# A gated delta-rule decoder layer: the inverse of the triangular blocks up to 16 rows by substitution on GpSimd, with the triangle in two buffers and a new order of steps

## What is computed

```python
def step(S, inp):
    qt, kt, vt, gt, bt = inp
    S = S * jnp.exp(gt)[..., None, None]
    kv = jnp.einsum('bhk,bhkv->bhv', kt, S)
    delta = (vt - kv) * bt[..., None]
    S = S + jnp.einsum('bhk,bhv->bhkv', kt, delta)
    o = jnp.einsum('bhk,bhkv->bhv', qt, S)
    return (S, o)
```

## Time and profile before

| | us |
|---|---|
| three runs: lowest, median, highest | 2253.6, 2258.28, 2272.47 |
| the profiled execution | 2256.81 |
| its span in the trace | 2255.0 |

### The profile page before, as it was taken

The page is one execution under the profiler, slowest core; times in us unless marked ns, Lnnn a source line. Parts: engine busy times, 40 slices in busy tenths (PEclk is TensorE's granted clock), DMA queues, the critical chain, the costliest instruction groups (busy, mean ns, idle before and its releaser), DMA issues.

```text
span 2255.0 us, 81282 instructions
## 1 busy us (share of the span) xinstructions
PE 2098.6 (93%) x33098; PEld 1805.4 (80%) x33130; DVE 1646.6 (73%) x5291; ACT 1385.5 (61%) x4262; POOL 803.3 (36%) x1845
## 2 busy tenths in 40 slices
...
DMA packets 25795, 30.66 MB, mean 14 GB/s; under 512 B 9264, under 2 KB 22592, under 8 KB 24656
## 3 DMA queue, kind: packets, MB, share of 16 engines
q1 hardware_dynamic: 25424, 25.46, 3.5%
...
## 4 chain that ended last, share of the span: by engine, by line
PE 83%; DVE 10%; issue 3%; SPq 2%; ACT 1%; POOL 0%; DMA 0%; DVEq 0%; POOLq 0%
PE bank_b L644 11%; PE bank_a L464 10%; PE bank_b L746 5%; PE bank_b L652 5%; PE bank_a L474 5%; PE bank_b L769 5%; PE bank_b L605 5%; PE bank_a L536 3%; PE bank_a L546 3%; PE bank_b L700 2%; PE bank_a L582 2%; PE bank_a L589 2%; PE bank_a L512 2%; DVE smax L1169 2%; PE bank_b L677 2%
## 5 line engine op out<-in xcount | busy, mean ns | idle before, releaser
L1021 DVE SCALAR_TENSOR_TENSOR acc<-ypad,convw,acc 128x128 f32<-128x128 f32 x1536 | 426.7, 346 | 109.4 <-ACT acc L823 109.4
L464 PE MATMUL bank_a<-xnT,wqkvz 128*128 128x128 f32 x2048 | 251.1, 279 | 27.2 <-DVE scoreT L1092 24.6
L464 PEld LDWEIGHTS bank_a<-xnT,wqkvz 128*128 128x128 f32 x2048 | 243.0, 195 | 36.6 <-issue 34.9
L1433 POOL TENSOR_SCALAR lnv<-mv 128x1 f32<-128x1 f32 x128 | 24.8, 193 | 582.9 <-DVE mv L1111 580.2
L934 ACT ACTIVATE prob<-bank_b,nmax 128x128 f32<-128x128 f32 x512 | 181.4, 382 | 6.7 <-DVE nmax L1171 4.2
L1387 POOL TENSOR_TENSOR ostat<-ostat 128x4 f32<-128x4 f32 x64 | 18.7, 293 | 456.3 <-ACT gseg L888 456.2
L914 ACT ACTIVATE prob<-bank_b 128x512 f32<-128x512 f32 x64 | 38.2, 597 | 211.7 <-PE bank_b L644 211.7
L1076 DVE TENSOR_TENSOR ablk<-bank_a,const 128x128 f32<-128x128 f32 x256 | 72.6, 284 | 105.7 <-PE bank_a L536 102.7
L823 ACT ACTIVATE acc<-bank_a,convw 128x128 f32<-128x128 f32 x512 | 147.9, 397 | 0.0
L644 PE MATMUL bank_b<-x2T,wg 128*128 128x128 f32 x1024 | 141.7, 296 | 0.0
L546 PE MATMUL bank_a<-ablk,xblk 32*32 32x32 f32 x8192 | 123.3, 195 | 15.6 <-DMA bk<-in_bk_dram 9.2
...
## 6 DMA issues: line engine op xcount, KB each, us to landing
xin<-in_x_dram SPq DMA_DIRECT2D x32, 128.0 KB, 2.4
cin<-in_ctx_dram SPq DMA_DIRECT2D x32, 128.0 KB, 2.8
out_dram<-yout SPq DMA_DIRECT2D x32, 128.0 KB, 1.7
...
```

The costliest lines, as they stand in the source:

```text
L464: last = mm(A[bank][:, b * P:(b + 1) * P], wqkvz[:, c, o:o + P], xnT[:, c, :], start=(c == 0), stop=(c == KC - 1))
L1021: stt(acc[:, c, :], ypad[:, c, k:k + P], convw[:, c, k:k + 1], acc[:, c, :], ALU.mult, ALU.add).then_inc(conv.sem, 1)
```

## The change

**Blocks up to 16 rows.** `a_init` and the levels s = 2, 4, 8 go, with their constants; level s = 16 stays (`a_la0`, `a_la1`, `a_lb0`, `a_lb1`). In their place comes a chain over four engines:

- DVE `a_lt`: the four diagonal blocks of kkT times a scale into diag (four instructions as in `a_init`).
- SP `a_l1`: diag to memory (l_mem). `a_l2`: four DMAs back into lsub, in which each partition holds one 16x16 block (64 blocks, each twice, once per half of the columns).
- POOL `a_sub0` to `a_sub2`: substitution, 15 steps of two instructions on 128 x (8 times 15, 14, ... 1) elements.
- SP `a_w1`: four DMAs of the result wsub to memory (z_mem); `a_w2`: back into zraw.
- DVE `a_zin`: two products with the scale into zin, two transposes into xblk.

The rows that these DMAs move hold 32 x 4 bytes (`a_l1`, `a_w2`; 1024 of them), 16 x 4 bytes (`a_l2`; 2048) and 8 x 4 bytes (`a_w1`; 2048).

```diff
+            def a_l1(n):
+                sp.wait_ge(*lt_ok(n))
+                sp.dma_start(l_mem.ap().rearrange("h p i -> p h i"), diag[:, :, :]).then_inc(l_saved.sem, 16)
...
+                        sp.dma_start(lsub[o:o + 32, :, :], sub_blocks(l_mem, w)).then_inc(l_in.sem, 16)
...
+            def substitute(n, part):
...
+                for j in range(5 * part, 5 * part + 5):
+                    w, rest = (wsub if j else sub_eye), SUB - 1 - j
+                    if j:
+                        pool.wait_ge(*sub_step(n, 2 * j))
+                    tt(tsub[:, 0:rest, :], lsub[:, j, j + 1:SUB].unsqueeze(2).to_broadcast([P, rest, HALF]),
+                       w[:, j, :].unsqueeze(1).to_broadcast([P, rest, HALF]), ALU.mult).then_inc(sub_step.sem, 1)
+                    pool.wait_ge(*sub_step(n, 2 * j + 1))
+                    tt(wsub[:, j + 1:SUB, :], w[:, j + 1:SUB, :], tsub[:, 0:rest, :], ALU.subtract).then_inc(sub_step.sem, 1)
```

**The order.** All lists are new, and SP has one:

```diff
+    act="b_rl@2 a_z0@1 a_sum b_sg0@2 a_z1@1 b_rt@2 a_mix3@1 b_sg1@2 a_xT a_ba a_ln a_qkv0 b_y1T@2 a_qkv1 "
+       "b_q@2 a_seg c_exp0 a_dec0 a_dec1 a_mix0 a_mix1 c_exp1 a_sq c_exp2 a_st c_exp3 c_pT0 c_pT1 a_zf@1 "
...
+    sp="a_l1@1 a_l2@1 c_out@4 b_in a_in@1 a_w1@1 a_w2@1".split(),
```

More of the change, by code:

```diff
@@ L112 @@
 ORDER = dict(
-    pe="a_lb10@1 a_la11@1 b_gu0@2 b_gu1@2 a_lb11@1 a_la20@1 b_gu2@2 b_gu3@2 b_dn0@2 a_la21@1 a_lb20@1 a_xT "
[3 rows of a table removed]
-       "b_oT0 b_oT1 c_pj1 b_w0 b_w1 a_la00 b_cT a_la01 a_lb00 a_vT0 b_v b_x2T a_lb01 a_la10 b_router".split(),
-    act="b_sum@2 b_cT@2 b_x2T@2 b_rl@2 b_sg0@2 b_rt@2 a_sum b_sg1@2 a_xT a_ba a_mix3@1 b_y1T@2 a_zf@1 b_q@2 "
-       "a_zo@1 c_exp0 a_mt@1 c_exp1 c_exp2 a_sz0@1 a_qkv0 a_sz1@1 c_exp3 a_o0@1 a_qkv1 a_o1@1 c_pT1 c_pT0 "
-       "c_R a_ln a_mix0 a_z1 a_mix1 a_z0 a_sq a_qkv2 c_y2T a_st c_h a_qkv3 c_lt c_c0 a_seg c_te c_wT c_c1 "
-       "a_dec0 a_dec1 b_oT0 b_oT1 a_mix2".split(),
-    dve="a_la11@1 a_lb10@1 a_la20@1 a_lb11@1 b_act0@2 a_xn a_conv32@1 b_act1@2 b_ys0@2 a_la21@1 a_lb20@1 "
[4 rows of a table removed]
-       "a_lb01 a_u0 b_top a_conv31".split(),
-    pool="b_rd@2 c_ln3@3 b_rt@2 a_x b_ln0@2 a_ga a_rq@1 b_y1b@2 a_osc0@1 a_osc1@1 a_g c_ln1 c_rx c_sig c_y2b "
-       "a_sc c_ln2 b_rs b_mask b_xh a_xr".split(),
+    pe="b_w1@2 b_cT@2 a_z1@1 a_vT0@1 a_qk@1 b_x2T@2 b_v@2 b_router@2 b_gu0@2 b_gu1@2 b_gu2@2 b_gu3@2 a_xT "
[3 rows of a table added]
+       "c_pj1 b_w0".split(),
+    act="b_rl@2 a_z0@1 a_sum b_sg0@2 a_z1@1 b_rt@2 a_mix3@1 b_sg1@2 a_xT a_ba a_ln a_qkv0 b_y1T@2 a_qkv1 "
+       "b_q@2 a_seg c_exp0 a_dec0 a_dec1 a_mix0 a_mix1 c_exp1 a_sq c_exp2 a_st c_exp3 c_pT0 c_pT1 a_zf@1 "
+       "a_zo@1 c_R a_mt@1 a_sz0@1 a_sz1@1 a_o0@1 a_o1@1 c_y2T c_h c_lt c_c0 c_c1 c_wT a_qkv2 a_qkv3 b_oT0 "
+       "b_oT1 c_te a_mix2 b_sum b_cT b_x2T".split(),
+    dve="a_u0@1 a_conv30@1 b_v@2 b_top@2 a_score@1 a_conv31@1 a_conv32@1 a_xn b_act0@2 b_act1@2 b_ys0@2 "
[3 rows of a table added]
+       "c_sum3 a_conv22 b_hid c_y3 b_x2".split(),
+    pool="a_x b_rd@2 b_rt@2 c_ln3@3 a_ga b_ln0@2 a_g b_y1b@2 a_rq@1 a_sc c_ln1 c_rx a_osc0@1 a_osc1@1 c_sig "
+       "c_y2b a_sub0 a_sub1 c_ln2 b_rs b_mask b_xh a_xr a_sub2".split(),
+    sp="a_l1@1 a_l2@1 c_out@4 b_in a_in@1 a_w1@1 a_w2@1".split(),
 )
```

295 lines of the change are left out of this document (165 added, 130 removed), and 13 rows, old and new, of tables (dve, pe).

## The result

| | before | after |
|---|---|---|
| median of 9 runs each, us | 2261.8 (2253.6 to 2272.47) | 2280.35 (2267.09 to 2287.71) |
| ratio, 95% interval | | 1.009 (1.007 to 1.011) |
| span of the profiled execution, us | 2255.0 | 2277.1 |

The change costs 0.9%. Forecast were 2288 us, in a range of 2215 to 2365. The total is close, but the profile shows that two terms of the sum were wrong and cancelled: the fit of the total is in good part luck. So the parts are worth more here than the sum.

The account below looks back on a forecast made before the run. PE's in-order list was taken as the bound. A trip: 59.5 us PE work, 6.7 new idle, 1.0 short waits, 1.05 code loading, 0.15 clock, so 68.4; +32 us over 32 trips on 2256.81 gave 2288, range 2215 to 2365.

Parts of the forecast that it names:

- gain of 141 us if nothing else bound: PE without twelve half steps: 4.4 us less work a trip, a trip of 61.7 us, 141 us over 32 trips.
- The list of ACT: ACT's in-order work from first exponent to end of `a_zo`: 15.5 us, so `a_mt` starts at S + 16.4 at the earliest.
- The work of PE beside it: PE's work from the end of the scores (S) to `a_mt`: 9.7 us, so PE must idle 6.7 us there.
- Elsewhere: Short new waits in the rest of the trip, at `c_s`, the exponent table and `c_wT`: 1.0 us, ends 0 to 2.2.
- Loading of code: Waits of PE that the profile does not explain: 1.3 us a trip, falling to 1.05 with fewer matmuls.
- The clock: PE may run at the low clock for some us in the new idle place, mostly beside ACT: 0.15 us a trip.
- rival 4: Clock stays low behind the idle place, slowing PE work behind `a_mt`: +2 us net, trip 70.4, 2353 us; chance 0.13.
- rival 2: Gain and new waits cancel: removed work worth 5.7 us, not 4.4; trip 67.1, 2247 us; chance 0.13.
- Start and drain: One more DMA and one wait in SP's setup, 0.4 to 2 us, fewer PE instructions in the drain; nothing net.
- PE idles 6 to 8 us: Sign of a right forecast: PE's idle time per trip, most of it between the decays' exponents (L553) and `a_mt`.
- rival 1: ACT's list hides more than counted and PE stays the bound: trip 64.4, 2161 us; chance 0.15.
- POOL and the round trip: Transfers through memory take 11 us, hidden within 13 us before POOL is free, and POOL's substitution 12.1 us; costed at nothing.

Follow-up runs that it names:

- half: The kernel before with the 12 half steps of levels 2, 4 and 8 left out on PE and DVE, nothing added; 2207.33 us.
- tl2: The kernel after with a one-column SiLU on ACT ahead of the fourth exponent bank, bringing two more table loads; 2370.27 us.
- both: fill20 and startq together, so idle matmuls on PE and the small bias loads issued by ACT; 2238.79 us.
- fill12: The kernel after with 12 unused 128x128 matmuls on PE behind the second exponent matmul of the decays, in the wait for zin; 2282.34 us.
- fill20: fill12 with 8 more idle matmuls on PE ahead of the matmuls on the squares (L532); 2248.38 us.
- startq: The kernel after with the 32 small loads of bq and bk issued by ACT and not by SP; 2275.2 us.

## Why the prediction was right, and where it was wrong

**What bounds the kernel before.** Right: PE in order. half shows 4.6 us of busy time per trip for the twelve half steps (4.4 in the sum). What my "gain of 141 us if nothing else bound" hid is that the half steps covered 1.9 us of waits and that the clock falls more often without them, which takes another 1.2; I named no work whose cover they were.

**The list of ACT.** Right, term by term. From the first exponent to the end of `a_zo` it takes 431.74 + 0.76 - 417.49 = 15.0 us (15.5 in the sum), `a_mt` starts at S + 16.05 with S = 416.59 (16.4), and `a_kk` at S + 5.7 (5.3). tl2 shows that it is critical. The wait for zin is 2.85 us (3.4).

**The work of PE beside it.** Too low. Idle time in that place is 2.85 + 0.17 + 0.18 + 0.41 = 3.6 us and not 6.7, so PE fills 12.4 us and not 9.7. 1.3 us of it is the low clock (L560 and the first L746 in the short trip); the rest was not split up. This is the term that was mis-sized: a trip is the list of ACT plus the work of PE outside that place, which the sum put at 59.5 - 9.7 = 49.8 us and which is 59.4 - (12.4 - 1.3) = 48.3.

**Elsewhere.** Waits of 1.2 us (0.47, 0.38 and 0.37 for y1T, kT and wT) against 1.0. PE's own work at full clock: 64.31 us in both, less its idle matmuls (L557 and L529, busy 90.9 and 65.6 us in 32 trips) of 4.9, is 59.4; the sum had 59.5.

```profile
1022.30:1088.70 66.40, 64.31 (x697) 55.76 (x694) 47.94 (x145) 45.25 (x134) 32.21 (x85) 1.00 0.09 15
```

A clean trip takes 66.0, where the sum had 67.2; before it took 66.1. That step failed by 1.2 us: 0.35 in the list of ACT, 0.85 outside it (there 1.5 us less work of PE than in the sum, 0.2 more of waits, and the rest in no term).

**Loading of code.** The step "1.3 x 0.81 = 1.05 a trip" failed twice. The page counts two matmul records for each float32 matmul (the 12 that fill12 adds are 24 records a trip), so 384 records a trip go and not 192, and the share left is 0.63. And in the kernel after almost nothing of it is seen: with the clock held up, a mean trip of fill20 (66.40 over the first 27) is 0.1 us above its clean one. In part the 1.3 us were the clock: over 29 trips PE's waits for nothing that the profile shows come to 19.8 us before (L536 10.5, L546 3.6, L644 3.3, L554 1.9, two of 0.5 together; L718 apart, which all trips have), 0.7 a trip. In half, which has the same number of matmuls as after and no new idle place ahead of `a_mt`, they come to 1.2 us. So they go with the fewer matmuls and need no idle place, and by far more than the share of 0.63 says. Why is not shown, nor that they are the loading of code.

**The clock.** I gave it 0.15 us, and rival 4 two. A mean trip is 67.38 - 66.0 = 1.4 us above a short one, and fill20 gives 1.0 of them back; so 1.0 us a trip is shown to be the clock, and the other 0.4 is argued. Rival 4 named the right thing at the wrong place: behind the wait for zin, and behind `a_mt`, the low clock is hidden or absent; it costs where it falls between the second wait (L532) and `a_mt`, up to 2.3 us.

**The trips together.** Forecast +1.0 us a trip, measured 0.0: 33 us too much. That is nearly the trip of rival 2 (67.1), but not by its way: the removed work was worth 4.6 busy us and not 5.7.

**Start and drain.** "One more DMA and one wait in SP's setup, 0.4 to 2 us" failed: +19.5 us in the start. These 19.5 and the 33 of the trips have opposite signs, and that is why the total fits: 2288.8 - 33 + 19.5 + 2.9 = 2278, against the 2278.91 of the profiled execution. I had read the new list of SP for the steady trip only. In the first trip `a_l1` and `a_l2` are issued behind the last of the weights, and the second x behind them and behind POOL's `a_xr`; before, it went ahead of the loop. That is one step of the diff moved past a queue, and both queues could be read. startq shows 8.3 us of it.

**The signs.** "PE idles 6 to 8 us" did not come: it idles 4.9 us in the short trip (66.00 - 61.09) and 5.9 in the long one (68.20 - 62.28), which is not under the 4 of rivals 1 and 2 either. The other signs of a right forecast came: ACT without a gap from the first exponent to `a_zo`, 7 table loads, `b_x2T` without a wait but once, 59.4 us of PE at full clock. Of rival 4, work at nearly twice its duration came, but ahead of `a_mt`.

**POOL and the round trip.** Diag ready to POOL free: 445.76 - 432.92 = 12.8 us (13 in the sum). In the short trip:

```profile
432.95 0.38 SPq L426 DMA_DIRECT2D lower_rows<-diag  x1
435.14 1.91 SPq L435 DMA_DIRECT2D lsub<-lower_rows  x4
```

```profile
445.76 0.39 POOL L1415 TENSOR_TENSOR tsub<-lsub,const 128x120 f32<-128x120 f32 x1
```

The first product of 128x120 takes 0.39 us and the difference 0.44 (0.44 each by the rate of the earlier trace rows). The legs take 6.2 us, from 432.95 to 437.05 + 2.1 = 439.15, where I took 11; the lower bound of 4.8 was the nearer one. The Trainium skill (DMA: Bandwidth & Descriptors, Specifications) says that transfers below 512 bytes are not at line rate and do read-modify-write; here that cost is not visible: rows of 128 and 64 bytes land in 2.3 and 2.1 us, the plain load of x in 2.4.

**GpSimd beside VectorE.** I weighed the rule of the Trainium skill (GPSIMD Engine Reference, Specifications), contention with VectorE instructions that read two SBUF inputs, against the earlier trace rows, and went by the rows. That was wrong as a reading and harmless in time: the rows stood beside small instructions of POOL (128x4). Beside products of 128x88 to 128x104 four taps take 1.72 in place of 1.11 us, which agrees with the rule.
